# Moving GpSimd's bias additions and weight selections in a fused conditional-projection and expert kernel

## The chip, the cores and the metric

The kernel runs on one core of one Trainium2 chip. The metric is the device time of one execution in microseconds (us). Before the change the median of 3 runs is 519.27 us (519.17 to 519.32). TensorE was granted its full clock throughout (mean 1.000).

## The reference, cut to what matters

Inputs are x (64 batches x 64 channels x 1024), 16 conditional 64x64 matrices, a base projection 1024x1024 with a bias, a gate for 8 experts, and for each expert a rank-16 pair lora_A, lora_B.

```
W = cond_weights[condition]                    # one 64x64 matrix for each batch
y = einsum('bct,bcd->bdt', x, W)
logits = y @ gate_w.T                          # 8 experts
weights, selected = top_k(logits, 2); weights = softmax(weights)
low = y @ lora_A.T                             # 8 x 16
out = x + (y @ base_w.T + base_b) + 2 * sum_e weight_e * (low_e @ lora_B_e.T)
```

Everything is float32.

## The kernel before

Two batches of 64 channels make a pair of 128 rows, so there are 32 pairs, and the kernel has one step for each. float32 precision comes from splitting each operand into a high and a low part of a faster type; a product is then three matmuls (high x high, high x low, low x high).

For pair s the work is this. ScalarE takes the high part of x, VectorE subtracts it to get the low part (`x_low`). GpSimd copies the two conditional matrices of the pair, both parts, into one diagonal tile `w_sel` (`select`, two copies, two buffers). TensorE multiplies (`mix`, 6 matmuls of 512 columns, in two halves `h`) into `mixed` in PSUM. ScalarE copies `mixed` in 16 pieces into `y_moved` (`move`; the semaphore `moved` counts one behind each 8 pieces, 2 for each pair from pair 2 on). VectorE transposes these in squares (`turn`, two instructions), ScalarE takes the high part `y_hi` and VectorE the low part `y_lo`. TensorE then projects with all of base, lora_A and gate at once: 8 blocks `k` x 3 products x 3 banks = 72 matmuls into `acc`.

Behind the projection VectorE computes the gate (`gating`: copy of the logits, `top`, `ties`, `below`, ... `chosen`, `scale`, `gate`, `low`), with one exponential on ScalarE (`gate_exp`). Beside the next pair's projection TensorE transposes `low` behind block k = 3 (`transpose_low`), ScalarE and VectorE split it (`lowT_hi`, `lowT_lo`), and behind block k = 5 TensorE adds the experts with 9 matmuls (`experts`, L590). `finish` on VectorE adds `acc` to `res`, which already holds x + bias, and SyncE stores it.

x + bias is GpSimd's (`add_bias`, L273), one 128x1024 addition for each pair. `res` and `x_sb` have four buffers each, so the bias of pair n waits for the store of pair n - 4, and the load of x for pair n + 4 waits on SyncE for a count of `sum_ready`.

Each engine runs its own program in the order in which it is written. A step s of VectorE is: `gating(s-1)`, `turn(s+1)`, `lowT_low(s-1)`, `y_low(s+1)` twice, `finish(s-1)`, `x_low(s+2)`. A step of ScalarE is: `gate_exp(s-1)`, `move(s+1)`, `lowT_high(s-1)`, `y_high(s+1)` twice, `x_high(s+2)`. A step of TensorE begins with `mix(s+1)`, then the projection of pair s.

The start is different. The weights (8 blocks of 128x1160) are split as they land: high parts on ScalarE (`w_high`, L352), low parts on VectorE (`w_low`, L487; the semaphore `w_ready` counts them). Step 0 on TensorE (`first_step`) follows block by block. In step 1 `mix(2)` stands behind block k = 1 of the projection. On VectorE `x_low(0, 2)` stands behind the last `w_low`, and then step 1 begins with `gating(0)`.

Of the kernel before, what the change touches and what calls it, by code (L numbers as in the profile page):

```python
# [19 lines left out]
def adaln_ffn_kernel(  # L20
# [29 lines left out]
    KT = T // P  # L50
    CONDITIONS = cond_w.shape[1] // CH
    assert cond_w.shape[0] == P
    PAIRS = B * CH // P
# [17 lines left out]
    with ExitStack() as ctx:  # L71
# [3 lines left out]
        def sem(name):  # L75
            return ctx.enter_context(nc.semaphore(name))
# [53 lines left out]
        w_ready = sem("w_ready")  # L130
# [16 lines left out]
        moved = sem("moved")  # L147
        turned = sem("turned")
        sel_ready = sem("sel_ready")
# [21 lines left out]
        sum_ready = sem("sum_ready")  # L171
# [13 lines left out]
        @block.sync  # L185
        def _(sp):
            sp.dma_start(cond_sb[:, :], condition).then_inc(cond_in, 16)

            def load_x(j, c):
                sp.dma_start(x_sb[:, c % 4, :], x_pairs[4 * j + c]).then_inc(x_in[c % 4], 16)  # L190

            load_x(0, 0)
            for k in range(KT):
                sp.dma_start(w_raw[:, k, :], w_blocks[k]).then_inc(w_in[k], 16)  # L194
                if k == 0:
                    load_x(0, 1)
            load_x(0, 2)
            sp.dma_start(bias[:, :], base_b.partition_broadcast(P)).then_inc(bias_in, 16)
            sp.dma_start(lb_raw[:, :], lora_b).then_inc(lb_in, 16)
            load_x(0, 3)  # L200

            def store(j, c):
                sp.wait_ge(res_ready, 4 * j + c + 1)
                sp.dma_start(out_pairs[4 * j + c], res[:, c % 4, :]).then_inc(stored[c % 4], 16)

            with sp.Fori(0, (PAIRS - 4) // 4) as j:
                for u in range(4):


                    sp.wait_ge(sum_ready, 4 * j + u + 3)  # L210
                    load_x(j, u + 4)
                    store(j, u)
            for n in range(PAIRS - 4, PAIRS - 1):
                store(0, n)

            last = PAIRS - 1
            sp.wait_ge(res_ready, PAIRS)
            sp.dma_start(out_pairs[last, :, 0:BW], res[:, last % 4, 0:BW]).then_inc(stored[last % 4], 16)
            sp.dma_start(out_pairs[last, :, 2 * BW:O], res[:, last % 4, 2 * BW:O]).then_inc(stored[last % 4], 16)
            sp.wait_ge(res_ready, PAIRS + 1)  # L220
            sp.dma_start(out_pairs[last, :, BW:2 * BW], res[:, last % 4, BW:2 * BW]).then_inc(stored[last % 4], 16)
            for i in range(4):
                sp.wait_ge(stored[i], 16 * (PAIRS // 4 + (2 if i == last % 4 else 0)))

        @block.gpsimd
        def _(pool):
            nc.gpsimd.memset(w_pair[:, :, :], 0.0).then_inc(w_zero, 1)
            nc.gpsimd.memset(w_sel[:, :, :, :].bitcast(F32), 0.0).then_inc(w_zero, 1)
            nc.gpsimd.memset(ident[:, :], 0.0).then_inc(ident_zero, 1)
            nc.gpsimd.memset(earlier[:, :, :], 0.0).then_inc(ident_zero, 1)  # L230
            pool.wait_ge(ident_zero, 2)
            for e in range(1, NE):
                nc.gpsimd.memset(earlier[:, e, 0:e], 1.0).then_inc(consts_ready, 1)
            nc.gpsimd.affine_select(out=ident[:, :], in_=ident[:, :], compare_op=ALU.not_equal, fill=1.0, base=0,
                                    pattern=[[-1, P]], channel_multiplier=1).then_inc(consts_ready, 1)

            def select_first(c):  # L240

                cond = pool.value_load(cond_sb[0:1, 2 * c:2 * c + 1], min_val=0, max_val=CONDITIONS - 1)
                nc.gpsimd.tensor_copy(w_pair[0:CH, c, 0:CH], cw[0:CH, bass.ds(cond * CH, CH)]) \
                    .then_inc(first_lower, 1)

            def select(j, c):

                n = 4 * j + c
                if c == 2:
                    pool.wait_ge(cw_ready, 1)  # L250
                else:
                    pool.wait_ge(sum_ready, n)

                pool.wait_ge(mix_done, 2 * n - 2)
                for b in range(2):
                    if b == 1:
                        pool.wait_ge(sel_ready, 2 * n - 3)
                    half = slice(b * CH, (b + 1) * CH)
                    cond = pool.value_load(cond_sb[0:1, bass.ds(8 * j + 2 * c + b, 1)], min_val=0,
                                           max_val=CONDITIONS - 1)  # L260
                    nc.gpsimd.tensor_copy(w_sel[half, c % 2, :, half], cw_parts[half, :, bass.ds(cond * CH, CH)]) \  # L261
                        .then_inc(sel_ready, 1)

            def add_bias(j, c):

                n = 4 * j + c
                if c >= 4:

                    pool.wait_ge(stored[c % 4], 16 * (j + c // 4))
                pool.wait_ge(x_in[c % 4], 16 * (j + c // 4 + 1))  # L270

                pool.wait_ge(sel_ready, 2 * n - 2 if c >= 3 else 2)
                nc.gpsimd.tensor_tensor(res[:, c % 4, :], x_sb[:, c % 4, :], bias[:, :], ALU.add).then_inc(sum_ready, 1)  # L273

            pool.wait_ge(cond_in, 16)
            pool.wait_ge(cw_in, 16)

            pool.wait_ge(w_zero, 2)
            select_first(0)
            select_first(1)  # L280
            pool.wait_ge(cw_hi_ready, 1)

            pool.wait_ge(first_lower, 2)
            nc.gpsimd.tensor_tensor(cw_parts[:, 1, :], cw[:, :], cw_parts[:, 0, :].bitcast(F32), ALU.subtract) \
                .then_inc(cw_ready, 1)
            select(0, 2)
            pool.wait_ge(bias_in, 16)
            for n in range(3):
                add_bias(0, n)
            select(0, 3)  # L290
            add_bias(0, 3)
            with pool.Fori(0, (PAIRS - 4) // 4) as j:
                for u in (4, 5, 6, 7):
                    select(j, u)
                    add_bias(j, u)

        @block.scalar
        def _(act):
# [416 lines left out]
```

## Time and profile before

| | us |
|---|---|
| median of 3 runs | 519.27 |
| the profiled execution's own time | 517.31 |
| its span (first to last instruction) | 515.6 |
| TensorE busy | 503.9 (98%) |
| VectorE busy | 343.8 (67%) |
| ScalarE busy | 266.5 (52%) |
| GpSimd busy | 103.2 (20%) |

Busy time is the time in which an engine had at least one instruction under way. A view in order of time gives the start of an instruction, its duration, and in brackets how long the engine was idle before it and what released it. PE is TensorE, DVE VectorE, ACT ScalarE, POOL GpSimd, SP SyncE. An instruction's duration includes time in which it waited for a port of the memory behind its engine's own start.

### The profile page before, as it was taken

To read this page: it belongs to the slowest core of one execution; us is meant where nothing else is said; L and a number is where in the kernel's file an instruction comes from. 1 tells how busy PE (TensorE), PEld (TensorE's weight loads), DVE (VectorE), ACT (ScalarE), POOL (GpSimd) and SP (SyncE) were. 2 spreads that over 40 slices of the span, in tenths; PEclk is the share of its full clock that TensorE was granted. 3 is DMA by queue.
4 is the path that set the end of the run, shared out by engine and by line. 5 is a ranking of instruction groups with operands and counts; after the bars stand their busy time and mean duration, and the time that the engine had idled before them with its cause. 6 is when DMAs were issued, how large, how long until landed. Compare 5 with 4: busy or idle time off the path is not lost.

```text
span 515.6 us, 8429 instructions
## 1 busy us (share of the span) xinstructions
PE 503.9 (98%) x2836; PEld 494.7 (96%) x2836; DVE 343.8 (67%) x678; ACT 266.5 (52%) x649; POOL 103.2 (20%) x112
## 2 busy tenths in 40 slices
PE   5998999999999999999999999999999999999997
PEld 5998999999999999999999999999999999999997
DVE  3997766767666767666767666767666667667544
ACT  4745446645446645456554456554456554466510
POOL 1672102222112222112221012221022221021000
PEclk9999999999999999999999999999999999999999
DMA  8712211222201222201222202222102222101112
GB/s 336 319 41 84 81 42 40 83 81 81 81 33 49 81 81 81 81 18 63 81 81 81 74 11 78 81 81 81 62 19 81 81 81 81 47 34 41 42 41 83
DMA packets 11100, 40.01 MB, mean 78 GB/s; under 512 B 1234, under 2 KB 1618, under 8 KB 11090
## 3 DMA queue, kind: packets, MB, share of 16 engines
q1 hardware_dynamic: 10946, 39.36, 20.8%
q10 hardware_dynamic: 144, 0.52, 0.3%
q8 instruction: 6, 0.10, 0.1%
q14 instruction: 4, 0.03, 0.0%
HBM read 23.10 MB, written 16.78 MB: 77 GB/s over the span
## 4 chain that ended last, share of the span: by engine, by line
PE 92%; DVE 4%; ACT 2%; DMA 2%; issue 1%; SPq 0%
PE acc L551 74%; PE acc L590 9%; PE mixed L577 8%; DVE w_lo L487 2%; DMA w_raw<-in_proj_w 2%; ACT y_moved L327 1%; PE mixed L584 1%; ACT w_hi L352 0%; DVE y_turned L411 0%; DVE ties L428 0%; DVE x_parts L415 0%; DVE y_lo L403 0%; ACT cw_parts L360 0%; SPq L194 0%; SPq L190 0%
## 5 line engine op out<-in xcount | busy, mean ns | idle before, releaser
L551 PE MATMUL acc<-w_hi,y_hi 128*128 128x388 f32 (+1 forms) x768 | 181.9, 342 | 0.0
L551 PE MATMUL acc<-w_lo,y_hi 128*128 128x388 f32 (+1 forms) x768 | 179.7, 339 | 1.0 <-DVE w_lo L487 1.0
L551 PE MATMUL acc<-w_hi,y_lo 128*128 128x388 f32 (+1 forms) x768 | 179.6, 338 | 0.0
L327 ACT COPY y_moved<-mixed 32x256 f32<-32x256 f32 x480 | 174.1, 363 | 5.6
L273 POOL TENSOR_TENSOR res<-x_sb,bias 128x1024 f32<-128x1024 f32 x32 | 79.7, 2494 | 303.8 <-DMA out<-res 301.9
L551 PEld LDWEIGHTS acc<-w_lo,y_hi 128*128 128x128 f32 x768 | 138.2, 188 | 1.3 <-DVE w_lo L487 1.3
L551 PEld LDWEIGHTS acc<-w_hi,y_lo 128*128 128x128 f32 x768 | 138.8, 188 | 0.0
L551 PEld LDWEIGHTS acc<-w_hi,y_hi 128*128 128x128 f32 x768 | 134.7, 188 | 3.4
L411 DVE STREAM_TRANSPOSE y_turned<-y_moved 128x512 f32<-128x512 f32 x60 | 69.0, 1186 | 63.8 <-ACT y_moved L327 63.8
L341 ACT ACTIVATE exps<-below 128x8 f32<-128x8 f32 x32 | 6.7, 209 | 176.0 <-DVE below L430 176.0
L480 DVE TENSOR_TENSOR res<-acc,res 128x776 f32<-128x776 f32 x31 | 30.0, 967 | 56.1 <-PE acc L590 56.1
L444 DVE SCALAR_TENSOR_TENSOR chosen<-rank,exps 128x8 f32<-128x8 f32 x32 | 58.1, 1815 | 1.3 <-DVE rank L440 0.3
L577 PE MATMUL mixed<-x_parts,w_sel 128*128 128x512 f32 x180 | 45.7, 389 | 0.0
L315 ACT CAST y_hi<-y_turned 128x512 fp32r<-128x512 f32 x60 | 37.4, 623 | 15.7 <-DVE y_turned L411 15.5
L403 DVE TENSOR_TENSOR y_lo<-y_turned,y_hi 128x512 fp32r<-128x512 f32 x60 | 39.5, 683 | 0.0
L415 DVE TENSOR_TENSOR x_parts<-x_sb,x_parts 128x1024 fp32r<-128x1024 f32 x30 | 38.7, 1288 | 0.0
L577 PEld LDWEIGHTS mixed<-x_parts,w_sel 128*128 128x128 f32 x180 | 33.5, 188 | 4.7
L590 PE MATMUL acc<-lb_hi,lowT_hi 128*128 128x388 f32 (+1 forms) x96 | 30.5, 318 | 1.9 <-DVE lowT_lo L465 1.9
L337 ACT CAST x_parts<-x_sb 128x1024 fp32r<-128x1024 f32 x30 | 31.4, 1048 | 0.1
L590 PE MATMUL acc<-lb_hi,lowT_lo 128*128 128x388 f32 (+1 forms) x96 | 30.6, 319 | 0.0
L590 PE MATMUL acc<-lb_lo,lowT_hi 128*128 128x388 f32 (+1 forms) x96 | 30.5, 318 | 0.0
L261 POOL CAST w_sel<-cw_parts 64x128 fp32r x60 | 18.5, 309 | 50.5 <-POOL res L273 25.7
(44 smaller groups left out, 238.8 us busy)
## 6 DMA issues: line engine op xcount, KB each, us to landing
x_sb<-in_x SPq DMA_DIRECT2D x32, 512.0 KB, 3.7
out<-res SPq DMA_DIRECT2D x31, 512.0 KB, 2.9
w_raw<-in_proj_w SPq DMA_DIRECT2D x8, 580.0 KB, 10.0
cw<-in_cond_w ACTq DMA_DIRECT2D x1, 512.0 KB, 3.5
bias<-in_base_b SPq DMA_DIRECT2D x1, 512.0 KB, 14.8
lb_raw<-in_lora_b SPq DMA_DIRECT2D x1, 512.0 KB, 15.6
out<-res SPq DMA_DIRECT2D x2, 194.0 KB, 2.0
out<-res SPq DMA_DIRECT2D x1, 124.0 KB, 2.0
```

Source lines behind the costliest of these rows:

```text
L273: nc.gpsimd.tensor_tensor(res[:, c % 4, :], x_sb[:, c % 4, :], bias[:, :], ALU.add).then_inc(sum_ready, 1)
L315: nc.scalar.copy(high, y).then_inc(y_hi_ready, 1)
L327: last = nc.scalar.copy(y_moved[q * SQ:(q + 1) * SQ, g, :], mixed[g * SQ:(g + 1) * SQ, h, q % 2 * TQ:(q % 2 + 1) * TQ])
L337: nc.scalar.copy(x_parts[:, 0, :], x_sb[:, c % 4, :]).then_inc(x_hi_ready, 1)
L403: nc.vector.tensor_tensor(low_part, y, high, ALU.subtract).then_inc(y_ready, 1)
L411: nc.vector.transpose(y_turned[:, :, ks, :], squares[:, :, ks, :]).then_inc(turned, 1)
L415: nc.vector.tensor_tensor(x_parts[:, 1, :], x_sb[:, c % 4, :], x_parts[:, 0, :].bitcast(F32), ALU.subtract).then_inc(x_split, 1)
L444: nc.vector.scalar_tensor_tensor(out=chosen[:, :], in0=rank[:, :], scalar=float(TOP_K), in1=exps[:, :], op0=ALU.is_lt, op1=ALU.mult).then_ ...
L480: return nc.vector.tensor_tensor(part, acc[:, c % 2, b, 0:BW], part, ALU.add)
L551: return nc.tensor.matmul(acc[:, c % 2, b, 0:hi - lo], y_part[:, c % 2, k, :], w_part[:, k, lo:hi], start=(k == 0 and product == 0), stop= ...
L577: last = nc.tensor.matmul(mixed[:, h, :], w_sel[:, c % 2, w_part, :], x_parts[:, x_part, h * 512:(h + 1) * 512], start=(w_part + x_part == ...
L590: last = nc.tensor.matmul(acc[:, c % 2, b, 0:hi - lo], low_part[:, :], lb_part[:, lo:hi], start=False, stop=(low_part is lowT_lo), skip_gr ...
```

## The change

Three things are edited. First, at the start, the biases of pairs 0, 1 and 2 stood one behind another, then came the selection for pair 3 and the bias of pair 3. Now the bias of pair 0 waits until all 8 low parts of the weights are done (`w_ready`), and the biases of 1, 2 and 3 stand each in a step of their own. Second, GpSimd's step n was: select for pair n, then bias of pair n. It is now: select for pair n + 2, then a wait until ScalarE has moved pair n + 1 (`moved` at 2n), then the bias of pair n. The last four steps are written out; the bias of pair 31 has no wait on `moved`. Third, SyncE's wait ahead of the load of x for pair n + 4 asks for n + 1 biases instead of n + 3.

```diff
--- before.py
+++ after.py
@@ -207,7 +207,7 @@
                 for u in range(4):
-                    sp.wait_ge(sum_ready, 4 * j + u + 3)
+                    sp.wait_ge(sum_ready, 4 * j + u + 1)
                     load_x(j, u + 4)
                     store(j, u)
             for n in range(PAIRS - 4, PAIRS - 1):
@@ -249,7 +249,8 @@
                 if c == 2:
                     pool.wait_ge(cw_ready, 1)
                 else:
-                    pool.wait_ge(sum_ready, n)
+                    pool.wait_ge(sum_ready, n - 2)
                 pool.wait_ge(mix_done, 2 * n - 2)
                 for b in range(2):
@@ -262,14 +263,9 @@
                         .then_inc(sel_ready, 1)
             def add_bias(j, c):
-                n = 4 * j + c
                 if c >= 4:
                     pool.wait_ge(stored[c % 4], 16 * (j + c // 4))
                 pool.wait_ge(x_in[c % 4], 16 * (j + c // 4 + 1))
-                pool.wait_ge(sel_ready, 2 * n - 2 if c >= 3 else 2)
                 nc.gpsimd.tensor_tensor(res[:, c % 4, :], x_sb[:, c % 4, :], bias[:, :], ALU.add).then_inc(sum_ready, 1)
             pool.wait_ge(cond_in, 16)
@@ -285,14 +281,28 @@
                 .then_inc(cw_ready, 1)
             select(0, 2)
             pool.wait_ge(bias_in, 16)
-            for n in range(3):
-                add_bias(0, n)
-            select(0, 3)
-            add_bias(0, 3)
-            with pool.Fori(0, (PAIRS - 4) // 4) as j:
+            pool.wait_ge(w_ready, KT)
+            pool.wait_ge(sel_ready, 2)
+            add_bias(0, 0)
+            def step(j, c, ahead=True, beside_turn=True):
+                if ahead:
+                    select(j, c + 2)
+                    pool.wait_ge(sel_ready, 8 * j + 2 * c + 2)
+                if beside_turn:
+                    pool.wait_ge(moved, 8 * j + 2 * c)
+                add_bias(j, c)
+            for n in (1, 2, 3):
+                step(0, n)
+            with pool.Fori(0, (PAIRS - 8) // 4) as j:
                 for u in (4, 5, 6, 7):
-                    select(j, u)
-                    add_bias(j, u)
+                    step(j, u)
+            for n in range(PAIRS - 4, PAIRS):
+                step(0, n, ahead=(n + 2 < PAIRS), beside_turn=(n + 1 < PAIRS))
         @block.scalar
         def _(act):
```

The instructions of TensorE, VectorE and ScalarE, and their order, are the same. On GpSimd, at the start behind the subtraction that makes `cw_parts`, the order before is this (COPY into `w_sel` is a select, TENSOR_TENSOR into `res` a bias; the first of the two selections of pair 2 is left out ahead of it):

```order
L261 COPY w_sel<-cw_parts 64x2x64
L273 TENSOR_TENSOR res<-x_sb,bias 128x1024 [waits sel_ready,x_in0,bias_in]
L273 TENSOR_TENSOR res<-x_sb,bias 128x1024 [waits sel_ready,x_in1]
L273 TENSOR_TENSOR res<-x_sb,bias 128x1024 [waits sel_ready,x_in2]
L259 TENSOR_LOAD cond_sb [waits mix_done,sum_ready]
L259 ISA x2
L261 ISA
L261 COPY w_sel<-cw_parts 64x2x64
```

and in the changed kernel, from the same place on:

```order
L262 COPY w_sel<-cw_parts 64x2x64
L269 TENSOR_TENSOR res<-x_sb,bias 128x1024 [waits sel_ready,x_in0,w_ready,bias_in]
L260 TENSOR_LOAD cond_sb [waits mix_done,sum_ready]
L260 ISA x2
L262 ISA
L262 COPY w_sel<-cw_parts 64x2x64
L260 TENSOR_LOAD cond_sb [waits sel_ready]
L260 ISA x2
L262 ISA
L262 COPY w_sel<-cw_parts 64x2x64
L269 TENSOR_TENSOR res<-x_sb,bias 128x1024 [waits x_in1,moved,sel_ready]
```

The three biases in a row have become one, and the first selection of pair 3 stands right behind it. In the loop, a step of GpSimd before (the second copy of a selection, then the bias) reads:

```order
L257 REGISTER_ALU
L259 ISA [waits sel_ready]
L259 TENSOR_LOAD cond_sb
L259 ISA x2
L261 ISA
L261 COPY w_sel<-cw_parts 64x2x64
L273 TENSOR_TENSOR res<-x_sb,bias 128x1024 [waits sel_ready,x_in2,stored2]
```

and the same place now:

```order
L258 REGISTER_ALU
L260 ISA [waits sel_ready]
L260 TENSOR_LOAD cond_sb
L260 ISA x2
L262 ISA
L262 COPY w_sel<-cw_parts 64x2x64
L269 TENSOR_TENSOR res<-x_sb,bias 128x1024 [waits stored2,x_in2,moved,sel_ready]
```

The kinds of instructions stand in the same order; what moved is the pair they belong to (the copy is now for a pair two further on than the bias) and the bias has the wait on `moved` in addition.

## Rows read from the trace of the kernel before

**Rows 1.** The page: busy time of each engine, share, instructions.
```profile
PE 503.9 (98%) x2836; PEld 494.7 (96%) x2836; DVE 343.8 (67%) x678; ACT 266.5 (52%) x649; POOL 103.2 (20%) x112
```
**Rows 2.** The chain of waits in order of time: start us, us, what.
```profile
29.91 2.06 DVE ties L428
...
38.29 2.12 DVE y_turned L411 x2
...
46.91 6.34 PE acc L551 x36
```
**Rows 3.** TensorE in order of time, around the start: start us, us, work [idle].
```profile
24.70 0.69 PE L551 MATMUL acc<-w_hi,y_hi 128*128 128x388 f32 x3
26.37 0.79 PE L551 MATMUL acc<-w_lo,y_hi 128*128 128x388 f32 x3 [0.98 <-DVE w_lo L487]
27.00 0.69 PE L551 MATMUL acc<-w_hi,y_lo 128*128 128x388 f32 x3
...
30.70 1.55 PE L577 MATMUL mixed<-x_parts,w_sel 128*128 128x512 f32 x6
...
38.14 0.70 PE L551 MATMUL acc<-w_hi,y_lo 128*128 128x388 f32 x3
40.72 0.42 PE L590 MATMUL acc<-lb_hi,lowT_hi 128*128 128x388 f32 x1 [1.89 <-DVE lowT_lo L465]
```
**Rows 4.** VectorE in order of time, around the start.
```profile
18.32 1.35 DVE L487 TENSOR_TENSOR w_lo<-w_raw,w_hi 128x1160 fp32r<-128x1160 f32 x1
19.60 0.68 DVE L403 TENSOR_TENSOR y_lo<-mixed,y_hi 128x512 fp32r<-128x512 f32 x1
...
22.75 3.56 DVE L487 TENSOR_TENSOR w_lo<-w_raw,w_hi 128x1160 fp32r<-128x1160 f32 x1
...
26.24 3.40 DVE L415 TENSOR_TENSOR x_parts<-x_sb,x_parts 128x1024 fp32r<-128x1024 f32 x1
```
**Rows 5.** GpSimd in order of time, around the start.
```profile
18.68 1.16 POOL L261 CAST w_sel<-cw_parts 64x128 fp32r x1 [0.72 <-POOL w_sel L261]
...
25.05 6.84 POOL L273 TENSOR_TENSOR res<-x_sb,bias 128x1024 f32<-128x1024 f32 x2
...
38.52 0.29 POOL L261 CAST w_sel<-cw_parts 64x128 fp32r x1 [0.82 <-POOL w_sel L261]
```
**Rows 6.** ScalarE in order of time, around the start.
```profile
32.15 0.21 ACT L341 ACTIVATE exps<-below 128x8 f32<-128x8 f32 x1 [8.34 <-DVE below L430]
32.27 5.99 ACT L327 COPY y_moved<-mixed 32x256 f32<-32x256 f32 x16
```
**Rows 7.** All engines in order of time, from one step in the middle.
```profile
263.23 1.52 PE L577 MATMUL mixed<-x_parts,w_sel 128*128 128x512 f32 x6
...
264.21 5.99 ACT L327 COPY y_moved<-mixed 32x256 f32<-32x256 f32 x16
...
264.67 2.39 POOL L273 TENSOR_TENSOR res<-x_sb,bias 128x1024 f32<-128x1024 f32 x1 [10.89 <-DMA out<-res]
264.75 0.22 DVE L440 TENSOR_REDUCE rank<-greater 128x8 f32<-128x64 f32 x1
265.00 2.09 DVE L444 SCALAR_TENSOR_TENSOR chosen<-rank,exps 128x8 f32<-128x8 f32 x1
...
270.23 2.31 DVE L411 STREAM_TRANSPOSE y_turned<-y_moved 128x512 f32<-128x512 f32 x2 [2.16 <-ACT y_moved L327]
...
272.48 0.24 DVE L465 TENSOR_TENSOR lowT_lo<-mixed,lowT_hi 128x128 fp32r<-128x128 f32 x1
...
272.64 1.33 DVE L403 TENSOR_TENSOR y_lo<-y_turned,y_hi 128x512 fp32r<-128x512 f32 x2
...
274.21 0.34 PE L590 MATMUL acc<-lb_hi,lowT_hi 128*128 128x388 f32 x1
...
277.03 1.22 DVE L415 TENSOR_TENSOR x_parts<-x_sb,x_parts 128x1024 fp32r<-128x1024 f32 x1
...
278.79 1.52 PE L577 MATMUL mixed<-x_parts,w_sel 128*128 128x512 f32 x6
```
## The prediction

> **What bounds the kernel now.** I read the busy times first. TensorE is busy 98% of the span and GpSimd 20% [rows 1], so a change of GpSimd's order can gain only where TensorE waits, or lose where it makes TensorE wait. Next the chain of waits in order of time: from 40.72 us on every piece is TensorE's own, matmul behind matmul, such as the 36 matmuls of 6.34 us that follow at 46.91 [rows 2]. A step in the middle lasts 278.79 - 263.23 = 15.56 us [rows 7] and has no wait of TensorE in it. Before 40.72 the chain goes through other engines: a comparison `ties` of 2.06 us, the 16 copies of `move`, two transposes of 2.12 us [rows 2]. So I turn to TensorE's own timeline there. It shows two waits that VectorE ends: for the last low part of the weights at 26.37, and for `lowT_lo` at 40.72 [rows 3].
>
> Their cost is read from starts, because the idle number leaves out the refilling of the pipeline. A group of three matmuls takes 6.34 / 36 x 3 = 0.53 us when nothing waits [rows 2]. The group behind 24.70 would start at 25.23 and starts at 26.37, and the next at 27.00, 0.63 later instead of 0.53 [rows 3]: 1.14 + 0.10 = 1.24 us lost. The experts would start at 38.14 + 0.53 = 38.67 and start at 40.72: 2.05 us lost.
>
> Both waits have GpSimd behind them. A low part of the weights takes 1.35 us; the last one, started at 22.75, takes 3.56, while the first bias runs until the second starts at 25.05 [rows 4, 5]. The low part of x at 26.24 takes 3.40 instead of 1.22 [rows 4, 7]. `ties` takes 2.06 us in the chain [rows 2] and ends when the third bias does, at 25.05 + 6.84 = 31.89 [rows 5]. These have two inputs in SBUF. It is a wait for a port and comes from the bias: in the middle `chosen`, two inputs in SBUF, takes 2.09 us and ends with the bias at 267.06, while a reduction with one input, started inside the same bias, takes 0.22 [rows 7].
>
> **The change, part by part.** Start, first wait. The bias of pair 0 now waits for all low parts. The last low part then takes 22.75 + 1.35 = 24.10 instead of 26.31 and is there before TensorE wants it at 25.23. TensorE gains the whole 1.24 us: `mix(2)` starts at 30.70 - 1.24 = 29.46 instead of 30.70.
>
> Start, second wait. At 24.10 bias 0 (2.39 us) and `x_low(2)` (1.22 us) want the port together. Whichever goes first, both are done by 24.10 + 2.39 + 1.22 = 27.7, and `mix(2)` wants x_low at 29.46. The logits can be taken from about 26.6, `ties` at 27.8 at the latest. Before, the exponential came 32.15 - 31.97 = 0.18 us behind the end of `ties` [rows 2, 6]; the gate's exponential is now done by 28.5. Biases 1 and 2 are gone from this place: bias 1 waits for the move. So `move(2)`, which began right behind the exponential at 32.27 [rows 6], now waits for the first half of `mix(2)` alone. In the middle a move began 264.21 - 263.23 = 0.98 us behind the start of its mix, also behind an exponential, so the half takes at most that [rows 7]; the least is half of the six matmuls' 1.55 us, 0.78 [rows 3]. The move starts between 29.46 + 0.78 = 30.24 and 30.44. From the start of the move to the experts it was 40.72 - 32.27 = 8.45 us, the copies (5.99), the transposes (2.12), `lowT_lo` and a wake-up [rows 2, 3, 6], and stays that. The experts start at 38.69 to 38.89 instead of 40.72, a gain of 1.83 to 2.03. I take 1.9. TensorE would be there at 38.67 - 1.24 = 37.43, so it still waits, and the 1.24 us of the first wait are not a second term: they are inside the 1.9, since the second wait ends on the chain through the move.
>
> The steps behind it. Their length is TensorE's 15.56 us, and the question is only whether the bias in its new place makes anything late. Take T as the end of a move and the start of the transposes (270.23) [rows 7]. I estimate that the bias starts at T + 0.1, or up to T + 0.6 if its waits and register work come one behind another, and so ends at T + 2.5 to T + 3.0. Beside it are the two transposes (2.31 us, one input), `lowT_lo` at T + 2.25 (one input in PSUM, one in SBUF), and from T + 2.41 the two `y_lo` (both in SBUF) [rows 7].
> - Transposes: their cost beside a bias is not in the trace. The nearest row is a selection at 38.52, wholly inside the transposes of 38.29 to 40.41: 0.29 us [rows 2, 5]. A like selection at 18.68, against a low part of the weights from 18.32, took 1.16 [rows 4, 5]. I take nothing. The upper bound is the whole bias, 2.39 us a step.
> - `lowT_lo`: a like form, `y_lo` out of PSUM at 19.60, took its 0.68 us although the selection from 18.68 was still running until 19.84 [rows 4, 5]. I take nothing; the bound is 0.6 us, and the slack is 274.21 - 272.72 = 1.49 [rows 7].
> - `y_lo`: delayed by up to 0.6 us, and hidden, since TensorE wants them only behind the next mix, at about 280.3, 6 us after they are done at 273.97 [rows 7]. If that cover were gone it would be 0.6 us a step.
> - Selections: two copies of 0.29 us, each behind some 0.8 us of idle (0.82 at 38.52 [rows 5]), so done by T + 3.0 + 2 x 1.1 = T + 5.2, or 275.4. `x_low` starts at 277.03 [rows 7]. They are wanted at the mix a step and more later.
> - Gain: `chosen` loses its 1.9 us of waiting in each step, which only gives slack to a chain that already had it. Nothing, since TensorE has no wait there.
> - Queue behind the wait on `moved`: the bias of pair n, then the selections of n + 3. The bias is wanted by `finish` in the next step, over 15 us later. SyncE asks for one bias more than the load's pair instead of three; the load stands in SyncE's queue behind the store of the pair before, which comes behind the experts, and bias n is done by then. Loads and stores keep their times. The first load (pair 4) may go earlier; nobody waits for it.
>
> The end. Biases 30 and 31 run one behind the other beside the last turn, and the port can hold the second `y_lo(31)` back until both are done at T + 5.0 or so, and `finish(29)`, which stands behind it, starts at T + 5.7 to T + 6.3. Without this it would start with the end of the 9 experts matmuls, at T + 3.98 + 9 x 0.18 = T + 5.6. TensorE wants both only behind the two blocks that follow the experts, 6 x 0.53 = 3.2 us after T + 5.6. Nothing.
>
> On the transposes the Trainium skill, page "SBUF — State Buffer", section "Who interferes with whom", says that a VectorE instruction with at most one SBUF input contends with GpSimd only in its two-port modes, but then for the whole of the other's instruction. The trace agrees for two SBUF inputs (2.09 us for `chosen`) and for the reduction. If the transposes ran in such a mode, that page's rule would make this change slow, and the rival below has its price.
>
> **Sum.** The profiled execution took 517.31 us, span 515.6. Less 1.9: span 513.7, own time 515.4. The median of the runs is 519.27, 1.96 above the profiled one, and I carry that over: 517.4 us, 0.37% less.
>
> **Rivals.**
> - Only little or nothing arrives (519.3; or 518.0 if the first wait's 1.24 us alone come through). Mechanism: bias 0 still lies on `ties`, so that the exponential, not the mix, starts the move. It decides if bias 0 ends later than 30.2. For it: this is what happened to the three biases. Against: it starts near 24.10 and the two port users need 3.6 us.
> - The transposes are blocked by the bias (slower). The bias starts first or between them, `lowT_lo` is then ready at T + 0.1 + 2.39 + 2.31 + 0.2 = T + 5.0, TensorE wants it at 274.21 - 270.23 = T + 3.98 less 0.1: 1.1 us in each of about 29 steps, 32 us, so 549 us. It decides from a delay of 1.4 us on; if each blocks only part, the time lies between. For it: no row shows a bias beside a transpose. Against: the selection of 0.29 us inside them.
> - The bias comes late and reaches `x_low`. `x_low` ends at 278.25 and mix's matmuls begin at 278.79, some 0.4 us of slack behind the pipeline [rows 7]. It decides if the bias starts later than T + 4.4; each step then loses up to 2.39 - 0.4 = 2.0 us, up to 577 us. A selection alone (0.29) stays within the slack. Against: nothing but `moved` and long finished semaphores stand before it.
>
> **How the numbers follow.** Forecast 76%, little or nothing 15% (3 of them at 518.0), blocked transposes 6%, a late bias 3%. The likeliest gives 517.4, its own range 517.2 to 517.5 by the bounds of the move's start, and a few tenths more for the wake-ups and the spread of a run. I extend it upward to take in the 518.0 case and most of the nothing case: 516.8 to 519.0. A measurement of this kernel tells about 0.2% (1.04 us) from no change. Faster by more: the forecast and the 518.0 case, 0.79. Within: the other 12 of the nothing case, and 1 of the slow ones for a delay that stays small, 0.13. Slower: 0.08.
>
> **What would show it.** Right: the last low part of the weights takes 1.35 us; TensorE has no wait near 25; the first move starts near 30.3, and the wait for the experts has shrunk from 1.89 to about 1.2 us of idle, near 38.8; steps of 15.56 us; transposes of 2.3 us with a bias inside them; `chosen` 0.17 us in all steps. Wrong: `lowT_lo` later than 1.4 us, new idle rows of TensorE before L590 or L577 in the loop, a move that still starts behind its exponential at the start, or a span that moves while the steps' length does not match 15.56.

## The result and the profile after

The changed kernel takes 516.27 us (median of 5 runs, 515.77 to 516.77), the kernel before 519.32 us (median of its 5 runs beside it, 519.17 to 519.81). The ratio is 0.9939, 95% interval 0.9924 to 0.9953: 3.1 us less. The forecast was 517.4 us, 1.9 us less, with a range of 516.8 to 519.0. The direction was right and the gain is 1.6 times the one forecast, outside the range.

The profiled execution of the changed kernel took 515.93 us, span 514.2. Its busy times answer to [rows 1]:

```profile
PE 503.7 (98%) x2836; PEld 495.0 (96%) x2836; DVE 284.2 (55%) x678; ACT 267.3 (52%) x649; POOL 107.3 (21%) x112
```

VectorE is busy 59.6 us less; that is `chosen`, which took 58.1 us over 32 steps and now takes 5.3. The group by line shows it (engine, tile, count, busy us, mean ns):

```profile
L454 DVE SCALAR_TENSOR_TENSOR chosen<-rank,exps 128x8 f32<-128x8 f32 x32 | 5.3, 167 | 1.4 <-DVE rank L450 0.3
```

Sixty microseconds of VectorE are worth nothing in themselves, as TensorE had no wait there. The gain is at the start. TensorE in order of time, to be held against [rows 3]:

```profile
25.09 0.69 PE L561 MATMUL acc<-w_hi,y_hi 128*128 128x388 f32 x3
25.62 0.69 PE L561 MATMUL acc<-w_lo,y_hi 128*128 128x388 f32 x3
...
29.85 1.54 PE L587 MATMUL mixed<-x_parts,w_sel 128*128 128x512 f32 x6
...
37.15 0.70 PE L561 MATMUL acc<-w_hi,y_lo 128*128 128x388 f32 x3
39.33 0.42 PE L600 MATMUL acc<-lb_hi,lowT_hi 128*128 128x388 f32 x1 [1.48 <-DVE lowT_lo L475]
```

The first wait is gone: the groups are 0.53 us apart through the last block of weights. The second is shorter, 39.33 - 37.15 - 0.53 = 1.65 us by starts instead of 2.05. Why is in the rows of the other engines, VectorE first, then ScalarE and GpSimd, against [rows 4, 5, 6]:

```profile
20.33 3.91 DVE L497 TENSOR_TENSOR w_lo<-w_raw,w_hi 128x1160 fp32r<-128x1160 f32 x3
24.16 1.22 DVE L425 TENSOR_TENSOR x_parts<-x_sb,x_parts 128x1024 fp32r<-128x1024 f32 x1
...
27.23 0.48 DVE L438 TENSOR_TENSOR ties<-logits_sb 128x64 f32<-128x64 f32 x1
```

```profile
27.89 0.21 ACT L351 ACTIVATE exps<-below 128x8 f32<-128x8 f32 x1 [4.54 <-DVE below L440]
30.74 6.01 ACT L337 COPY y_moved<-mixed 32x256 f32<-32x256 f32 x16 [2.64 <-PE mixed L587]
```

```profile
24.38 3.26 POOL L269 TENSOR_TENSOR res<-x_sb,bias 128x1024 f32<-128x1024 f32 x1 [4.41 <-DVE w_lo L497]
28.35 0.30 POOL L262 CAST w_sel<-cw_parts 64x128 fp32r x1 [0.71 <-POOL res L269]
```

The last three low parts take 3.91 us together. `x_low` goes first and takes its 1.22, the bias waits (3.26 us instead of 2.39), and `ties` waits only for its tail. The exponential is done 2.6 us before the move, which now waits for the mix.

A step in the middle, all engines, against [rows 7]:

```profile
261.84 1.52 PE L587 MATMUL mixed<-x_parts,w_sel 128*128 128x512 f32 x6
...
268.86 2.34 DVE L421 STREAM_TRANSPOSE y_turned<-y_moved 128x512 f32<-128x512 f32 x2 [4.10 <-ACT y_moved L337]
269.09 2.41 POOL L269 TENSOR_TENSOR res<-x_sb,bias 128x1024 f32<-128x1024 f32 x1 [10.82 <-ACT y_moved L337]
...
271.11 0.26 DVE L475 TENSOR_TENSOR lowT_lo<-mixed,lowT_hi 128x128 fp32r<-128x128 f32 x1
...
272.82 0.34 PE L600 MATMUL acc<-lb_hi,lowT_hi 128*128 128x388 f32 x1
...
277.40 1.52 PE L587 MATMUL mixed<-x_parts,w_sel 128*128 128x512 f32 x6
```

The step is 15.56 us as before. The bias starts at T + 0.23 and lies over both transposes, which take 2.34 us instead of 2.31; `lowT_lo` takes 0.26 instead of 0.24.

Between the two profiles the experts moved from 40.72 to 39.33, 1.39 us, and the spans differ by 1.4. The medians differ by 3.05. So the profiled executions explain less than half of what the runs show, and the experiments are about the rest.

### The profile page after: what moved, and what is told of

Read it like the earlier page. It is cut to its first block, busy times and chain, and to the rows that moved or that the text cites. A ratio compares the mean times of both kernels' runs of the same rounds, so it can differ in the third digit from the quotient of the medians.

```text
span 514.2 us, 8424 instructions
## 1 busy us (share of the span) xinstructions
PE 503.7 (98%) x2836; PEld 495.0 (96%) x2836; DVE 284.2 (55%) x678; ACT 267.3 (52%) x649; POOL 107.3 (21%) x112
## 4 chain that ended last, share of the span: by engine, by line
PE 97%; ACT 1%; DMA 1%; DVE 1%; DVEq 0%; issue 0%
PE acc L561 78%; PE acc L600 9%; PE mixed L587 8%; PE mixed L572 2%; ACT y_moved L337 1%; DMA cw<-in_cond_w 1%; PE mixed L594 1%; DVE y_turned L421 0%; DVEq L505 0%; DVE res L493 0%; DVE w_pair L506 0%; DVE lowT_lo L475 0%; DVEq L506 0%; DVEq L502 0%
## 5 line engine op out<-in xcount | busy, mean ns | idle before, releaser
L269 POOL TENSOR_TENSOR res<-x_sb,bias 128x1024 f32<-128x1024 f32 x32 | 78.6, 2458 | 323.1 <-ACT y_moved L337 318.7
L413 DVE TENSOR_TENSOR y_lo<-y_turned,y_hi 128x512 fp32r<-128x512 f32 x60 | 42.0, 731 | 0.0
L425 DVE TENSOR_TENSOR x_parts<-x_sb,x_parts 128x1024 fp32r<-128x1024 f32 x30 | 36.5, 1216 | 0.0
L262 POOL CAST w_sel<-cw_parts 64x128 fp32r x60 | 23.6, 393 | 50.0 <-POOL res L269 24.4
L358 ACT CAST lowT_hi<-mixed 128x128 fp32r<-128x128 f32 x32 | 8.5, 266 | 34.7 <-PE mixed L594 34.7
```

The lines of the kernel that those rows point to most:

```text
L413: nc.vector.tensor_tensor(low_part, y, high, ALU.subtract).then_inc(y_ready, 1)
L425: nc.vector.tensor_tensor(x_parts[:, 1, :], x_sb[:, c % 4, :], x_parts[:, 0, :].bitcast(F32), ALU.subtract).then_inc(x_split, 1)
```

## The experiments

**The kernel before, once more.** No edit.

> The kernel before, unchanged, timed again beside itself and profiled once more. The changed kernel's runs gained 3.05 us in the median, but its profiled execution only 1.4 us over the one before (515.93 against 517.31), because the one of before lies 2 us under that kernel's own other runs (519.17 to 519.81). Theory A (the start varies): in most executions of before the port between VectorE and GpSimd is taken in another order at the start, and the execution is 2 us longer inside its span. Then this profile, if its time is near 519.3, shows a span near 517.6, the experts' first matmul at 42 to 43 instead of 40.72, and steps of 15.56 us. Theory B (the loop varies): span near 517.6, experts still near 40.7, and steps that lose time now and then. Theory C (outside the span): span 515.6 and 3.7 us around it. Under all three the ratio is 1.000.

Measured: 519.09 against 519.00 us, ratio 1.0002 (0.9994 to 1.0011). The profiled execution took 518.96 us, span 517.2. Of the 34 runs of this kernel in that comparison, 32 have spans of 517.1 to 517.6 and two have 515.5 and 515.6. The profile shown ahead of the prediction (span 515.6) is of the rare kind; this one is of the usual kind. TensorE, VectorE, GpSimd in order of time:

```profile
25.00 0.80 PE L551 MATMUL acc<-w_lo,y_hi 128*128 128x388 f32 x3 [1.34 <-DVE w_lo L487]
28.46 0.80 PE L551 MATMUL acc<-w_lo,y_hi 128*128 128x388 f32 x3 [1.60 <-DVE w_lo L487]
32.80 1.54 PE L577 MATMUL mixed<-x_parts,w_sel 128*128 128x512 f32 x6
...
42.24 0.42 PE L590 MATMUL acc<-lb_hi,lowT_hi 128*128 128x388 f32 x1 [1.45 <-DVE lowT_lo L465]
```

```profile
21.38 3.56 DVE L487 TENSOR_TENSOR w_lo<-w_raw,w_hi 128x1160 fp32r<-128x1160 f32 x1
...
24.87 3.54 DVE L487 TENSOR_TENSOR w_lo<-w_raw,w_hi 128x1160 fp32r<-128x1160 f32 x1
```

```profile
21.07 2.64 POOL L273 TENSOR_TENSOR res<-x_sb,bias 128x1024 f32<-128x1024 f32 x1 [1.33 <-DMA bias<-in_base_b]
```

and, from the profile ahead of the prediction, the same bias:

```profile
21.53 3.56 POOL L273 TENSOR_TENSOR res<-x_sb,bias 128x1024 f32<-128x1024 f32 x1 [1.70 <-DMA bias<-in_base_b]
```

The first bias starts at 21.07, as soon as the bias row has landed, and that is 0.3 us before the seventh low part (21.38). It holds up that one, and the second bias holds up the eighth: 3.56 and 3.54 us. In the rare kind the first bias started at 21.53, just behind the seventh low part, and had to wait itself (3.56 us instead of 2.39). Which order comes is a race, the landing of the bias row against VectorE's start of the seventh low part. In the usual order TensorE waits twice for a low part instead of once, and the experts start at 42.24. Against the changed kernel's 39.33 that is 2.91 us. This is theory A, with theories B (the loop) and C (outside the span) out: the steps are 15.56 us in both, and 518.96 - 517.2 lies around the span, as 517.31 - 515.6 did.

The second wait is another one here than in the rows ahead of the prediction. VectorE's `ties`, then ScalarE:

```profile
31.94 0.22 DVE L428 TENSOR_TENSOR ties<-logits_sb 128x64 f32<-128x64 f32 x1
```

```profile
32.33 0.21 ACT L341 ACTIVATE exps<-below 128x8 f32<-128x8 f32 x1 [8.97 <-DVE below L430]
33.68 6.01 ACT L327 COPY y_moved<-mixed 32x256 f32<-32x256 f32 x16 [1.14 <-PE mixed L577]
```

By the time of `ties` the three biases are over (GpSimd's last ends at 30.66), so `ties` takes 0.22 us and not 2.06, and the move waits for the mix, 1.35 us behind the exponential, as it does in the changed kernel. The experts' wait is 1.45 us of idle here and 1.48 in the changed kernel. So in the usual kind the change gains nothing at `ties`: all of its gain is the two late low parts.

**The loop alone.** Start of before, loop of the changed kernel.

```diff
-            pool.wait_ge(w_ready, KT)
             pool.wait_ge(sel_ready, 2)
-            add_bias(0, 0)
+            for n in range(3):
+                add_bias(0, n)
+            select(0, 3)
+            pool.wait_ge(sel_ready, 4)
+            add_bias(0, 3)
+            select(0, 4)
+            select(0, 5)
...
-            for n in (1, 2, 3):
-                step(0, n)
```

> The start of before (biases 0, 1, 2 in a row as soon as the bias has landed, selection 3, bias 3), then the loop of the changed kernel (bias of pair n beside the turn of n + 1, selections two pairs ahead). Theory A (all of the gain is at the start): 519.3, ratio 1.000. Theory B (part of it is in the loop, where biases are no longer released by a store's landing): about 517.7, ratio 0.997. Both: the first wait for the low part of the weights and the wait for the experts are there as before.

Measured: 519.43 us, ratio 1.0009 (1.0001 to 1.0018), spans 517.4 to 517.8. None of the gain is in the loop. It may even be slower by 0.1%, at the edge of the interval. Of the 0.5 us between the spans of the two profiles (517.7 and 517.2), 0.27 stand already at the experts of step 1 (42.51 and 42.24), ahead of the loop, and the steps are 15.56 us; whether the rest is more than spread stays open.

**The wait on `moved` undone in the loop.** Start of the changed kernel.

```diff
-                    step(j, u)
+                    step(j, u, beside_turn=False)
...
-                step(0, n, ahead=(n + 2 < PAIRS), beside_turn=(n + 1 < PAIRS))
+                step(0, n, ahead=(n + 2 < PAIRS), beside_turn=False)
```

> The changed kernel without the wait on moved from pair 4 on: the bias of pair n runs right behind the selection for n + 2, some 3 us behind the head of step n - 1, beside the gating of VectorE, and the start is that of the changed kernel. Theory A: 516.3, the same as the changed kernel (0.994 of before), since TensorE never waits in the loop either way. Theory B: 517.7 (0.997) if a bias beside the gating costs something.

Measured: 517.23 us, ratio 0.9962 (0.9949 to 0.9975), neither of the two numbers. The profile (span 515.4) is 1.2 us longer than that of the changed kernel. 0.7 of it stand already at the experts of step 1 (40.04), where the two kernels run the same instructions: the start varies by such amounts from execution to execution (more below). The other 0.5 come once, where the loop begins without the wait, and a bias runs on right behind the selections. (From the experts of step 1 to the end of the span it is 475.4 us here, 475.2 in the run with the loop alone and 474.8 to 475.0 in all other profiles.) GpSimd and VectorE:

```profile
72.48 2.41 POOL L269 TENSOR_TENSOR res<-x_sb,bias 128x1024 f32<-128x1024 f32 x1 [0.26 <-POOL w_sel L262]
```

```profile
74.07 1.90 DVE L425 TENSOR_TENSOR x_parts<-x_sb,x_parts 128x1024 fp32r<-128x1024 f32 x1
```

`x_low` takes 0.68 us longer than its 1.22 and TensorE has its only wait in the loop there (0.24 us of idle ahead of the mix at 76.23). From then on TensorE waits for nothing: in a step in the middle the bias lies at 266.84, behind the gating and ahead of the transposes. So the wait on `moved` keeps a bias off `x_low` once, at the head of the loop; it brings no time of its own.

**One wait added to the kernel before.**

```diff
             pool.wait_ge(bias_in, 16)
+            pool.wait_ge(w_ready, KT)
             for n in range(3):
                 add_bias(0, n)
```

> The kernel before with one wait added: the three biases at the start wait until all low parts of the weights are done. Loop and selections as before. The first wait of TensorE near 26 goes (1.24 us), but the three biases now run from 24.1 to about 32.5 (3 x 2.39 and 1.22 of x_low between them) and still lie on ties, which ends near 32.5 instead of 31.97. By the chain through the exponential and the move, the experts then start at about 41.2, and the profile is 0 to 0.5 us longer than the profile of before (517.3 to 517.8). Theory A beyond that: if the other 2 us of the ordinary runs come from an order at the start in which the first bias lies on two low parts instead of one, this wait takes them away too, and the runs come at 517.3 to 517.8, ratio 0.997. Otherwise 519.3 or more.

Measured: 515.93 us, ratio 0.9953 (0.9938 to 0.9969), lower than both expectations. Spans: four of 513.8 to 514.2, two of 515.8 and 516.0. In the profile (514.1) the three biases in a row do not hold up `ties`, as I expected, but the instruction behind it:

```profile
27.15 0.41 DVE L429 TENSOR_TENSOR ties<-logits_sb 128x64 f32<-128x64 f32 x1
27.48 2.37 DVE L431 TENSOR_SCALAR below<-logits_sb,top 128x8 f32<-128x8 f32 x1
```

```profile
29.89 0.21 ACT L342 ACTIVATE exps<-below 128x8 f32<-128x8 f32 x1 [6.37 <-DVE below L431]
30.66 6.01 ACT L328 COPY y_moved<-mixed 32x256 f32<-32x256 f32 x16 [0.56 <-PE mixed L578]
```

`ties` got the port between the first and the second bias, `below` waited for the second, and the exponential still came 0.77 us before the mix half that starts the move. One line gives the whole gain of the change in four of six runs. A second profile of this kernel (its expectation below; time 517.05 us, span 514.4, `below` 2.37 us, exponential at 30.07 and move at 31.04) was again of the short kind by its span, so what the two long runs are was not seen; that in those `ties` loses the port to the second bias and `below` to the third is argued only.

> One more look at e3, whose runs were of two kinds: spans of 513.8 to 514.2 four times, and 515.8 and 516.0. Account: in the long kind ties loses the port to the second bias and below to the third, the exponential comes near 32.2 instead of 29.89, later than the mix half at 30.66, and the move and the experts are 1.6 to 1.8 us later. If this profile is of the long kind it shows that; if it is of the short kind (4 in 6), it looks as e3 and says nothing of the long one.

**The race fixed.** The same wait, for 6 low parts instead of 8: `pool.wait_ge(w_ready, KT - 2)`.

> The kernel before with one wait: the three biases wait until 6 of the 8 low parts of the weights are done (the other edit waited for all 8). Theory A (an order race at the start: a bias that starts just ahead of the seventh low part holds up two low parts, 517.2 us of span; one that starts just behind it holds up only the last, 515.6): VectorE goes on to the seventh at once and has the port, so the bias always holds up only the last one. Then every run, not 2 of 23, is of the short kind: span 515.6, TensorE waits once for a low part, the experts start near 40.7, time 517.4, ratio 0.997. If the 1.6 us between the two kinds come from elsewhere (landing of the weights, the loop), the runs stay at 519.0.

Measured: 517.51 us, ratio 0.9975 (0.9964 to 0.9986). Six of seven spans are 515.6 or 515.7, one 517.2 (its mean granted clock was 0.997, against 0.999 or 1.000 in the six, so whether it is the other order is open); of before, in the same comparison, one of 17 is 515.6. The profile has the waits of [rows 3]: mix at 30.70, experts at 40.72. A wait that only makes the first bias come second turns the usual kind into the rare one.

**The race worsened.** The bias row loaded ahead of x of pair 2.

```diff
-            load_x(0, 2)
             sp.dma_start(bias[:, :], base_b.partition_broadcast(P)).then_inc(bias_in, 16)
+            load_x(0, 2)
```

> The kernel before with two loads swapped at the start: the bias row is loaded ahead of x of pair 2, and lands some 1.3 us earlier (its 512 KB at about 400 GB/s). Theory A: the first bias then starts near 19.9, ahead of the sixth low part (20.1), and three low parts are held up instead of two: each costs 2.4 us less what TensorE had in hand, the last low part is done near 31.0 instead of 28.4, the experts start near 44.8, span 519.7, time 521.5, ratio 1.005. If x of pair 2 is what matters, it lands later by 1.3 us and ScalarE splits it later, but x_low stands behind the low parts anyway: no effect. Other theory (the loop or the landing of the weights makes the difference): 519.0.

Measured: 521.04 us, ratio 1.0036 (1.0025 to 1.0046), span 519.4; nine of the ten spans are 519.2 to 519.5 and one is 517.4. The bias starts at 20.19, 0.9 us earlier than in the usual kind and just ahead of the sixth low part (20.23), and TensorE waits three times:

```profile
23.87 0.80 PE L551 MATMUL acc<-w_lo,y_hi 128*128 128x388 f32 x3 [0.61 <-DVE w_lo L487]
27.33 0.80 PE L551 MATMUL acc<-w_lo,y_hi 128*128 128x388 f32 x3 [1.61 <-DVE w_lo L487]
30.79 0.79 PE L551 MATMUL acc<-w_lo,y_hi 128*128 128x388 f32 x3 [1.61 <-DVE w_lo L487]
```

Held-up low parts 0, 1, 2, 3 go with profiled spans of 514.2 (the changed kernel), 515.6, 517.2 and 519.4 us. This is what shows the cause: the number of held-up low parts was moved down to one, with the wait for six, and up to three, with the earlier load, and the time went with it.

**Mix(2) at the head of step 1**, in the changed kernel.

```diff
-                if c >= 2:
-                    mix(j, c + 1)
+                mix(j, c + 1)
...
-                    if k == 1 and c == 1:
-
-                        mix(j, c + 1)
```

> The changed kernel, with mix(2) at the head of step 1 like in all other steps, not behind block k = 1. Its x_low is done at 25.4 in the profile of the changed kernel, and TensorE comes to the place at 26.7. The mix then runs from 26.7 instead of 29.85, the move starts behind the exponential at about 28.1 instead of 30.74, and lowT_lo is ready at about 36.6, ahead of TensorE's 37.7. If the chain mix half, move, transposes, lowT_lo is what is left of the second wait (my account of the changed kernel), the wait for the experts (1.48 idle, 1.65 by starts) vanishes: span 512.6, time 514.6, ratio 0.991. If something else ends that wait, nothing changes against the changed kernel (516.3).

Measured: 513.86 us, ratio 0.9900 (0.9885 to 0.9916), span 512.1, better than the kernel before and the changed one. ScalarE and TensorE:

```profile
27.77 0.21 ACT L351 ACTIVATE exps<-below 128x8 f32<-128x8 f32 x1 [4.44 <-DVE below L440]
27.89 5.99 ACT L337 COPY y_moved<-mixed 32x256 f32<-32x256 f32 x16
```

```profile
37.28 0.34 PE L600 MATMUL acc<-lb_hi,lowT_hi 128*128 128x388 f32 x1
```

The wait for the experts is gone, and with it the 1.65 us. The experts start 2.05 us earlier than in the changed kernel; the 0.42 beyond the wait are an earlier start of TensorE in this execution (its second early group at 11.41 instead of 11.83). The medians of the two, timed beside each other, are 1.98 apart, 0.33 more than the wait. What was left of the second wait was the chain from the mix.

**The changed kernel again.**

> The changed kernel again, beside the kernel before and the three others on the same chip: 516.3, ratio 0.994. Theory A: its spans have one kind only, 514.0 to 515.0, since one bias alone, behind the last low part, can hold up nothing that TensorE waits for.

Measured: 515.84 us, ratio 0.9937 (0.9924 to 0.9951), spans 513.9 to 514.8.

**The one-line wait with the mix at the head.** The wait for all 8 low parts and the mix at the head of step 1, both in the kernel before.

> The kernel before with the wait for all 8 low parts ahead of its three biases (as e3) and mix(2) at the head of step 1 (as e6), so that against e6 only the places of biases 1 to 3, the selections and the loop differ. Account: in e3 the exponential came at 29.89, behind below, which took 2.37 us beside the second bias; it cost nothing there, since the mix half came at 30.66. In e6 the exponential at 27.77 is what starts the move. So here the move starts near 30.0 instead of 27.9, lowT_lo is done near 38.3, TensorE is there at 37.3 and waits 1.0 to 1.3 us: span 513.3, time 515.0, ratio 0.992, some 1.1 us above e6. In a share of the runs (2 of 6 in e3) the third bias lies on below or ties as well, and these are 2 us longer. If the spread of biases 1 to 3 is worth nothing even here, the time is e6's 513.9.

Measured: 515.49 us, ratio 0.9940 (0.9922 to 0.9958); the profiled span is 513.4, 1.3 us above the 512.1 with the biases spread. The exponential comes at 29.76 and the move right behind it:

```profile
29.88 6.00 ACT L328 COPY y_moved<-mixed 32x256 f32<-32x256 f32 x16
```

```profile
38.49 0.42 PE L591 MATMUL acc<-lb_hi,lowT_hi 128*128 128x388 f32 x1 [0.94 <-DVE lowT_lo L466]
```

So spreading biases 1 to 3, the other half of the change at the start, is worth nothing in the changed kernel, long kind apart, and 1.3 us as soon as the mix does not hide it. One of the seven runs has a span of 515.9, again the long kind; the changed kernel had none in ten runs.

## Why the prediction was wrong

By its own steps:

- **First wait, 1.24 us: right for the execution it was read from.** The last low part is ready in time and the wait is gone. The starts of TensorE's second early group, in the profile before, the changed kernel and the usual execution of before, are these:

```profile
11.44 3.91 PE L562 MATMUL mixed<-w_pair,x_sb 128*128 128x128 f32 x16
```

```profile
11.83 3.91 PE L572 MATMUL mixed<-w_pair,x_sb 128*128 128x128 f32 x16
```

```profile
11.28 3.91 PE L562 MATMUL mixed<-w_pair,x_sb 128*128 128x128 f32 x16
```

  From there to the mix it takes 30.70 - 11.44 = 19.26 us, 29.85 - 11.83 = 18.02 and 32.80 - 11.28 = 21.52. The first two differ by 1.24 to the digit; the third by 3.50, which is what the two waits of the usual execution cost.
- **Second wait: right in mechanism for that same execution, and only there.** Port conflict gone, exponential early, move started by the mix half, which came 0.89 us behind the mix's start (0.78 to 0.98 was the bound). The experts came at 39.33, not 38.69 to 38.89. 0.39 us of this is a later start of TensorE in that execution (the early group at 11.83 instead of 11.44), 0.14 the way from the move to the experts (8.59 instead of 8.45), of which the transposes beside the bias are 0.11. In the usual execution of before there was no conflict on `ties` to remove. So against most runs of before, only the account of the first wait carried the forecast; that the account of the second pointed the same way was luck.
- **The loop: right.** 15.56 us a step, transposes 2.34 us under a bias, `y_lo`, `lowT_lo`, selections and loads without cost, `chosen` without gain. Neither slow rival came.
- **The sum: wrong, and this is the step that failed.** "The median of the runs is 519.27, 1.96 above the profiled one, and I carry that over." I took the 1.96 us as something outside the kernel's waits that any version would have. Most of it was one more wait of TensorE at the start: in all but a few executions the first bias holds up one low part more (spans of 517.2 against 515.6). The kernel that waits for all low parts loses this too: its median lies 0.34 us above its profiled execution (516.27 and 515.93), not 1.96. The forecast of 517.4 less these 1.62, plus the 0.52 by which the gain between the profiled executions (1.38) fell short of 1.9, gives 516.3. With the usual execution as the base, the experts' 42.24 less 38.8 would have given 3.4 us and 515.8; the runs came at 516.27.

The signs were in what I had. The runs of before lay within 0.15 us of each other and 1.9 us above the profiled one, which points to a second kind of execution and not to spread. And the first bias of the profile started where a race could turn: it waits for a load, and VectorE's next low part starts within half a microsecond of the landing. I priced the port conflict in the order that the trace showed, not in the other one.

What was proposed as the main rival, that little arrives because bias 0 still lies on `ties`, happened in part (0.48 us instead of 0.21) and cost nothing.

## What to carry to other kernels

When the profiled execution lies clearly apart from runs that agree among themselves, take it for another kind of execution until shown otherwise: look for a race in it, here at the start, and price the change against both orders. An engine off the critical path that starts work on the landing of a load, beside an engine on the critical path with which it shares a port, is such a race. Here one wait on the critical engine's counter ended it, and in four of six runs did all the work of a larger rearrangement. Stalls taken from an engine that nobody waits for (60 us of VectorE in the loop) are worth nothing. But one that is hidden by another chain can begin to count when that chain is shortened: with the mix moved forward, the 2.37 us of `below` cost 1.3.

## What the runs showed that I had not expected

- `below`, a TENSOR_SCALAR of 128x8 with one tensor input in SBUF, took 2.37 us beside a bias in three profiles, while a TENSOR_REDUCE with one input (0.22) and the transposes (2.34 for two) went on beside one. I had ordered the conflicts by the number of inputs in SBUF. The Trainium skill, page "SBUF — State Buffer", section "Who interferes with whom", names `tensor_scalar` among the operations that can enter a two-port mode and then contend. The trace agrees that it contends, even at 8 elements a partition; that such a mode is the reason (and not, say, the scalar, which is read from SBUF too), no run shows.
- The port goes back and forth: in the repeated profile of before, biases in a row and low parts in a row took turns (3.56 and 3.54 us for low parts of 1.35, then 3.42 for the 1.22 of `x_low`), and in the profile ahead of the prediction likewise from the last low part on (3.56, then 3.40 for `x_low`); neither engine ran twice while the other waited.
- The start of one kernel varies by some tenths: mix(2) began at 29.85 and 29.91 in two profiles of the changed kernel and at 30.59 in one that differs from it only from pair 4 on. The 0.7 us arise before 12.6: TensorE's second early group starts at 12.57 there and at 11.83 in the changed kernel, and in both it is 18.02 us from there to the mix. The two groups of three matmuls ahead of it took 1.17 and 0.92 us instead of 0.68 and 0.69, at a granted clock of 1.00 in both; why is open. A kernel whose low parts come late does not show this: with the wait for six low parts the group started at 12.28, in the profile ahead of the prediction at 11.44, and the mix at 30.70 in both.
